# Two-layer cross-attention and mixture-of-experts kernel: the key rotation of layer 0 begun one step earlier, the routing weights laid out over 112 rows

## What is computed

```python
x = x + L0_xattn(layernorm(x), ctx)      # rotary on queries and on the context keys
x = x + L0_ffn(layernorm(x))             # 16 experts, 4 chosen per token, and one shared expert
x = x + L1_xattn(layernorm(x), ctx)      # rotary on the context keys only
x = x + L1_ffn(layernorm(x))             # 8 low-rank experts, 2 chosen per token

kv_r   = ctx * cos + rotate_half(ctx) * sin            # once per context
scores = (q_r @ kv_r.T) ; attn = softmax(scores)
out    = (attn @ kv_r) ...                             # values are the rotated context too

cw  = weight of each expert for each token             # zero for experts not chosen
acc = sum over e of cw[:, e] * (silu(x @ g_e) * (x @ u_e)) @ d_e
```

## Time and profile before

| what | value |
|---|---|
| median of 3 runs | 3447.54 us (3446.84 to 3452.19) |
| the profiled execution, its time | 3445.47 us |
| its span from first to last instruction | 3443.7 us |
| PE busy | 2980.6 us, 87% of the span |
| DVE busy | 2033.7 us, 59% |
| POOL busy | 1769.7 us, 51% |
| ACT busy | 1261.3 us, 37% |
| DMA engines, mean | 72 GB/s |
| mean granted clock of PE | 0.918 of full speed |

### The profile page before, as it was taken

One profiled execution on the slowest core, in us unless ns is written; L12 is line 12 of the kernel. 1 busy time (PEld: TensorE's weight loads), 2 busy tenths in 40 slices (PEclk: granted clock), 3 DMA queues, 4 the chain that ended last, 5 costly groups with the idle time before them and its releaser, 6 DMA issues. The chain is left out here.

```text
span 3443.7 us, 43529 instructions
## 1 busy us (share of the span) xinstructions
PE 2980.6 (87%) x16008; PEld 1691.6 (49%) x16008; DVE 2033.7 (59%) x2351; ACT 1261.3 (37%) x1747; POOL 1769.7 (51%) x1008
## 2 busy tenths in 40 slices
PE   7688978899888989888897789986997699888987
PEld 6444446444464444654445544453445444454445
DVE  3576656766467664676655556455645566446645
ACT  3124434244341444333443334332442244323432
POOL 0466723676436775366672247523771177315750
PEclk9789989899988999898998889988998899988998
DMA  7423213233114231132321233203321322122310
GB/s 253 118 61 87 62 40 92 72 81 81 34 60 110 63 84 50 61 101 57 74 58 50 88 77 76 74 6 86 78 52 51 86 60 67 53 61 67 83 56 6
DMA packets 117806, 247.54 MB, mean 72 GB/s; under 512 B 30415, under 2 KB 82879, under 8 KB 110038
## 3 DMA queue, kind: packets, MB, share of 16 engines
q1 hardware_dynamic: 117590, 244.57, 26.6%
HBM read 171.24 MB, written 48.27 MB: 64 GB/s over the span
## 5 line engine op out<-in xcount | busy, mean ns | idle before, releaser
L1215 POOL TENSOR_TENSOR sums<-sums,prob 125x896 f32<-125x896 f32 x528 | 1119.8, 2121 | 174.8 <-ACT prob L1102 125.0
L1331 DVE TENSOR_REDUCE maxpart<-pair 112x2 f32<-112x1000 f32 x720 | 861.5, 1197 | 464.1 <-PE pair L851 464.1
L1102 ACT ACTIVATE prob<-wide 125x896 f32<-125x896 f32 x768 | 704.3, 917 | 886.5 <-PE wide L877 884.5
L892 PE MATMUL single<-prob,kv 125*64 125x448 f32 x3072 | 758.1, 572 | 0.9
L872 PE MATMUL wide<-qhigh,kparts 64*125 64x448 f32 x3072 | 461.6, 378 | 0.0
L851 PE MATMUL pair<-kparts,qhigh 64*112 64x500 f32 x1440 | 358.3, 494 | 61.5 <-DVE maxpart L1331 47.3
L851 PEld LDWEIGHTS pair<-kparts,qhigh 64*112 64x112 f32 x1440 | 129.3, 176 | 489.8 <-DVE maxpart L1331 399.8
L1215 POOL TENSOR_TENSOR sums<-prob 125x896 f32<-125x896 f32 x64 | 134.4, 2100 | 408.4 <-ACT prob L1102 408.4
L872 PEld LDWEIGHTS wide<-qhigh,kparts 64*125 64x125 f32 x3072 | 283.3, 187 | 110.3 <-issue 81.2
L877 PE MATMUL wide<-shift,ones_row 64*125 64x448 f32 x1536 | 290.2, 373 | 48.8 <-DMA shift<-maxrow 48.8
L872 PE MATMUL wide<-qlow,kparts 64*125 64x448 f32 x1536 | 288.3, 370 | 0.0
(11 more groups left out here) (322 smaller groups left out, 4268.9 us busy)
## 6 DMA issues: line engine op xcount, KB each, us to landing
kparts<-keys_merged SPq DMA_DIRECT2D x64, 750.0 KB, 9.0
wexp_low_values<-in_experts SPq DMA_DIRECT2D x68, 384.0 KB, 3.1
kparts<-kparts SPq DMA_DIRECT2D x96, 250.0 KB, 3.1
keys_merged<-kparts SPq DMA_DIRECT2D x32, 750.0 KB, 7.6
recip<-zrec_merged SPq DMA_DIRECT2D x112, 112.0 KB, 2.8
raw<-in_ctx SPq DMA_DIRECT2D x33, 375.0 KB
w_low_values<-w_merged SPq DMA_DIRECT2D x64, 192.0 KB, 3.1
values_merged<-kv SPq DMA_DIRECT2D x32, 375.0 KB
```

The costliest lines, as they stand in the source:

```text
L892: mm = pe.matmul(mix_acc[64 * half:64 * half + DC, 0:HQ], kv[:, j % 3, t, :], prob[:, (j * LT + t) % NPROB, half * HQ:(half + 1) * HQ], st ...
L1102: nc.scalar.activation(prob[:, n_ % NPROB, :].rearrange("p (a b) -> p a b", a=2), acc[0:LP, :, 0:HQ], ACT.Exp)\
L1215: nc.gpsimd.tensor_tensor(dst, first_in, prob[:, n_ % NPROB, :], ALU.add).then_inc(s["pool_sum"], 1)
L1331: V.tensor_reduce(maxpart[:, j % 2, t:NMAX:4, b], acc[0:TQ, :, 0:LB], AX.X, ALU.max).then_inc(*R.signal_drained(kind, *key))
```

## The change

Four things are changed. (1) `rotate` for sequence 2 stays at t = 0 of tile 0; for sequences 3 to 7 it stands at t = 11 of the tile before, ahead of that step's `score` and thus ahead of the `mix` of t = 10. (2) `ropecos` goes from t = 1, 2 to t = 0, 1, and `rope` from t = 3, 4 to t = 2, 3. (3) `stash` goes from t = 9 to t = 11. (4) The second copy in cwT and pick goes from rows 32 to 47 to rows 96 to 111, so that the matmul of `weight` runs over 112 rows.

```diff
@@ -33,6 +33,7 @@
 MT = -(-HID // 128)
+CWLOW = 96
 ZP, ZC = 56, 8
@@ -134,8 +135,10 @@
         for t in range(LT):
             ahead = (j + 1, t + EARLY_MAX) if t + EARLY_MAX < LT else (j + 2, t + EARLY_MAX - LT)
-            if layer == 0 and t == 0 and j + 2 < BG:
-                add("rotate", j + 2)
+            if layer == 0 and t == 0 and j == 0:
+                add("rotate", 2)
+            if layer == 0 and t == LT - 1 and j + 3 < BG:
+                add("rotate", j + 3)
@@ -152,7 +155,7 @@
             if layer == 0 and t in (5, 6, 7) and j + 2 < BG:
                 keys(j + 2, t - 5)
-            if layer == 0 and t == 9 and j + 2 < BG:
+            if layer == 0 and t == LT - 1 and j + 2 < BG:
                 add("stash", j + 2)
@@ -160,10 +163,10 @@
             if t == 10 and j:
                 add("share", j - 1, 2)
-            if layer == 0 and t in (1, 2) and j + 2 < BG:
-                add("ropecos", j + 2, t - 1)
-            if layer == 0 and t in (3, 4) and j + 2 < BG:
-                add("rope", j + 2, t - 3)
+            if layer == 0 and t in (0, 1) and j + 2 < BG:
+                add("ropecos", j + 2, t)
+            if layer == 0 and t in (2, 3) and j + 2 < BG:
+                add("rope", j + 2, t - 2)
@@ -303,7 +306,7 @@
-        pick = sb("pick", [32 + E0, E0], F32R)
+        pick = sb("pick", [CWLOW + E0, E0], F32R)
@@ -358,7 +361,7 @@
-                for r in (0, 32):
+                for r in (0, CWLOW):
                     nc.vector.tensor_copy(pick[r:r + E0, :], ident[r:r + E0, r:r + E0])
@@ -549,7 +552,7 @@
-        cwT = buf("cwT", [32 + E0, NT], F32R)
+        cwT = buf("cwT", [CWLOW + E0, NT], F32R)
@@ -935,7 +938,7 @@
-                        pe.matmul(acc[:, 0:NT], c["pick"][:, i - 1:i].broadcast_to([32 + E0, 128]), cwT[:], start=True, stop=True)\
+                        pe.matmul(acc[:, 0:NT], c["pick"][:, i - 1:i].broadcast_to([CWLOW + E0, 128]), cwT[:], start=True, stop=True)\
                             .then_inc(*R.signal_filled(kind, *key))
@@ -1303,7 +1306,7 @@
-                        V.tensor_tensor(cwT[32:32 + E0, :], acc[0:E0, 0:NT], cwT[0:E0, :].bitcast(F32), ALU.subtract).then_inc(*R.signal_drained(kind))
+                        V.tensor_tensor(cwT[CWLOW:CWLOW + E0, :], acc[0:E0, 0:NT], cwT[0:E0, :].bitcast(F32), ALU.subtract).then_inc(*R.signal_drained(kind))
```

## The result

The changed kernel takes 3398.28 us (median of 4 runs, 3391.51 to 3399.68), the kernel before, run beside it, 3447.53 (3446.84 to 3452.19). The ratio is 0.985 with a 95% interval of 0.9833 to 0.9867: 49.2 us faster, where 43.9 were forecast. The profiled execution took 3397.9 us.

What follows compares the result with a forecast made beforehand. PE, busy 87% of the span, was taken as the bound, so only its standing still or slow stepping counted. -27.9 - 16 = -43.9 us took 3445.5 to 3401.6, median 3403.5; range 3394 to 3421.

Steps and rivals of the forecast that it cites:

- Part 1: Layer 0 attention loops: `ropecos` and `rope` one step earlier remove 24 PE waits for kv, -27.9 us.
- The tightest place: The pair of t = 4 needs the reduction of t = 3, queued behind the first `rope` half: 0.1 us early.
- the other bound: Attention loops: reductions ending 0.35 too late, 24 times, would give back 8.4 us and leave 19.5.
- Clock: Tile starts: PE may run partly at half clock; which starts are hit is drawn anew, +-5 us.
- Part 2: Tile end: `rotate` ahead of POOL's addition of t = 10 gives 0; DVE's sum waits 0.35 us in tile 0.
- Rival (c): Tile end: POOL becomes the bound if the rotation takes over 4 us; net +18, 3466 us; chance 0.04.
- Rival (a): Attention loops: `rope` halves sit out a full POOL addition, the earlier rope's gain is lost; 3431.5 us; chance 0.06.
- Part 3: SP's queue: moving `stash` from t = 9 to t = 11 leaves its order unchanged, 0 us.
- Part 4: Layer 0 experts: 112 rows in place of 48 save 0.41 us per expert, partly lost to late hid_low; -16 us.
- the chain: Experts: ACT's gate and up through to hid_low, 0.12 us late for PE; takes back about 1.3 per group.
- The sum: Whole kernel: -27.9 - 16 = -43.9 us, from 3445.5 profiled to 3401.6, median 3403.5.

Runs made afterwards that it cites:

- rope alone: The kernel before with `ropecos` and `rope` one step earlier and nothing else: 3413.17 us, ratio 0.9898.
- Both halves together: The changed kernel with both halves of `rope` at t = 2 in place of t = 2 and 3: 3468.3 us, ratio 1.0064.
- late context load: The changed kernel with SP's 375 KB load of the next context issued behind `stash` instead of after the third keyT: 3381.52 us, ratio 0.9807.
- the last run: The version with the late context load, with `rotate` put back to the head of the next tile: 3366.42 us, ratio 0.9766.

## Why the prediction was right

The forecast stood at 3403.5, the range at 3394 to 3421; 3398.3 was measured. Its steps:

- **Part 1, -27.9.** Right as a mechanism and nearly in size. The steps t = 5 to 6 gave 28.8. The tightest place held, with more room than thought: the first half took 1.08 and not 1.34, the reduction ended 0.41 before the pair and not 0.1, and none of the 8.4 of the other bound was given back. The rope alone measured 34.6, 6.7 above the term.
- **Clock, +-5.** The term was put at 0 in the mean, and it was not. The first two steps of the tiles are 6.0 shorter in the changed kernel's profile (and 2.4 in the rope's own), and that is no even draw. In the six kernels with the earlier rope and the context load where it was, these steps sum to 165.7 to 172.4 us, with 2 to 6 of the sixteen starts below full clock; in the three with the rope where it was, to 174.8 to 176.6, with 7 to 9. These are single profiled executions, but the two sets don't overlap. So part of what the rope gave beyond its term is fewer slow tile starts; why they become fewer is not shown. The working of the term has a slip as well: with levels of full and half, a mean of 0.66 over 5 us is two thirds of it at half clock and costs 1.7 us, not a third and 1.5. The seven slow starts in the profile before take 6.4 to 8.4 us for their two steps where the others take 5.3.
- **Part 2, 0.** Right: ratio 0.9999 alone, and 3397.7 with it taken out of the change. The wait was 0.21 against 0.35, and the pair missed nothing. Rival (c) needed a rotation of over 4 us; it took 2.0. Rival (a) didn't come about either: each half sat out the rest of an addition and not a whole one, and took 1.08 or 1.35. But "0" holds only while the division's DMA is late. With that DMA on time the same move costs 15 us. The prediction named the cover as time to spare in front of L1365; the one that mattered was in front of `ctx_n`.
- **Part 3, 0.** Right, for the reason given.
- **Part 4, -16.** Mis-sized: -12.1. The 0.41 per expert and the 1.3 per group for the chain came out (3.7 saved per 13 experts, 4.0 forecast; five waits of the load queue for hid_low in the first group, 1.5 together). The step that failed is that it stopped counting at the thirteenth expert. The chain that was late by 0.1 to 0.4 inside the run is late by 0.73 more at the last `down`, where PE has nothing else: 2.9 us in four groups. The remaining 1.4 of the 4.3 behind the stretches is within what that stretch scatters.
- **The sum** was 5.3 short, and that it came so near is in part luck: two errors of opposite sign. By the runs of the single parts the rope gave 6.7 more than its term (4.7 with the rotation moved as well) and the rows 3.9 less, together 46.7. The other 2.5 up to 49.2 lie within the intervals, which reach 4 to 6 us to either side of each of these numbers.

Of the expectations for the experiments two were off in size. Both halves together should have cost about 1.2 per tile and cost 2.9 (70 us over 24 tiles): the wait was 1.9, as the second half met nearly a whole addition, and the half-clock stretches behind it were not in the estimate. The late context load gave 17 by the medians in place of 27 to 37, as the wait that takes its place was not looked for on DVE; the last run shows that it was the rotation. Two more lay just outside their ranges: the rope alone (3413.17, expected 3414 to 3420) and 80 rows (3400.03, expected 3391 to 3400).

## What to carry to other kernels

A wait of PE for DVE's product is removed by one step's earlier entry, but look between which reductions each piece falls: one piece per gap was free, two cost 70 us. Where matmuls of few rows stand among full ones, compare the distances of starts; padding the contraction with zero rows can be cheaper than fewer rows. A move that costs nothing is free under the present timing only, so test it again after the next bottleneck has gone: here two edits that were good or neutral on their own collided.

## What the runs showed of the hardware

- A 448-column matmul of 48 rows between such of 128 costs 0.41 us in and out; with 80 and with 112 rows it costs nothing (0.01 at most).
- A DVE operation with two SBUF inputs of 125x384 takes 0.55 with POOL idle. If POOL adds when it begins, it ends 0.41 or 0.42 behind the end of that addition, in all 48 rope halves of the changed kernel: 1.06 to 1.35 each, and 3.46 for two in a row. `ctx_n` (128x448) takes 0.62, 1.25 or 2.07, by what it meets on POOL.
- A small store behind a 375 KB load in SP's queue may be read back after 3.91 us, without the load ahead of it after 1.40.
- After PE had stood still for 1.9 us in the middle of a tile, its granted clock fell to the lower level (0.66 over 5 us) in nine of 24 cases and stayed at full in fifteen. At the tile starts 2 to 9 of sixteen were below full as long as the wait at the tile's end was there, and none in the two kernels with the late context load.
